# Moving one pair of ScalarE copies from the odd to the even step of a fused GRU and FFN kernel

## The reference

```
gi = x_t @ W_ih + b_ih ; gh = h @ W_hh + b_hh           # 3 gates of 512
r, z = sigmoid(i_r + h_r), sigmoid(i_z + h_z)
n = tanh(i_n + r * h_n) ; h = (1 - z) * n + z * h       # 64 steps in sequence
qx, sx, sc = quantise(h[:, up_index])                   # row max, scale, round to FP8
t = silu(qx @ Wg.T * ...) * (qx @ Wu.T * ...)           # 1408 columns
qt, st, sct = quantise(t) ; y = qt @ Wd.T * ...
out = x + y
```

## Time and profile before

| | |
|---|---|
| median of the runs | 2902.66 us |
| the profiled execution | 2908.95 us, its span 2907.2 us |
| TensorE (PE) busy | 2569.9 us, 88% |
| VectorE (DVE) busy | 1682.8 us, 58% |
| GpSimd (POOL) busy | 1240.1 us, 43% |
| ScalarE (ACT) busy | 1141.0 us, 39% |
| mean granted TensorE clock | 0.960 of full speed |

### The profile page before, as it was taken

One profiled execution on the slowest core, in us unless ns is written; L12 is line 12 of the kernel. 1 busy time (PEld: TensorE's weight loads), 2 busy tenths in 40 slices (PEclk: granted clock), 3 DMA queues, 4 the chain that ended last, 5 costly groups with the idle time before them and its releaser, 6 DMA issues. The chain is left out here.

```text
span 2907.2 us, 154632 instructions
## 1 busy us (share of the span) xinstructions
PE 2569.9 (88%) x67605; PEld 1678.1 (58%) x67605; DVE 1682.8 (58%) x3398; ACT 1141.0 (39%) x2317; POOL 1240.1 (43%) x598
## 2 busy tenths in 40 slices
PE   2088999999889999998999999999996999999995
PEld 1066777776768888886664564745542444444442
DVE  8852222226622222226628778877483888888886
ACT  1312222225622222225603333323233777777773
POOL 0255666662156666662160450704501333333333
PEclk8599999999999999999999999999997999999997
DMA  6833222224422222226463352443522232322321
GB/s 192 237 84 79 73 70 73 73 73 116 129 62 72 71 73 71 71 73 174 135 155 113 99 161 85 137 147 95 165 93 91 66 93 80 94 83 86 91 57 51
DMA packets 234843, 293.74 MB, mean 101 GB/s; under 512 B 69581, under 2 KB 194023, under 8 KB 233895
## 3 DMA queue, kind: packets, MB, share of 16 engines
q1 hardware_dynamic: 212743, 240.84, 29.6%
q10 hardware_dynamic: 18304, 36.19, 3.6%
q0 software_dynamic: 3680, 15.21, 1.8%
HBM read 231.61 MB, written 60.45 MB: 100 GB/s over the span
## 5 line engine op out<-in xcount | busy, mean ns | idle before, releaser
L1145 PE MATMUL psum<-second_shared 64*32 64x384 f16 x32768 | 1026.9, 324 | 52.3 <-issue 33.8
L1153 PE MATMUL psum<-low_w,low_hot 64*32 64x384 f16 x16384 | 758.7, 324 | 3.2 <-issue 3.2
L1372 DVE TENSOR_SCALAR second_shared<-psum 32x384 f16<-32x384 f32 x496 | 272.3, 549 | 747.7 <-PE psum L1145 740.4
L953 POOL TENSOR_TENSOR low_hot<-first_shared,sum_mask 128x1024 f16<-128x1024 f16 x256 | 500.4, 1955 | 468.8 <-DVE first_shared L1359 196.1
L1145 PEld LDWEIGHTS psum<-second_shared 64*32 64x32 f16 x32768 | 562.7, 93 | 201.5 <-issue 94.6
L947 POOL TENSOR_TENSOR second_shared<-first_shared,whole_mask 128x2048 f16<-128x2048 f16 x128 | 462.7, 3615 | 456.1 <-PE psum L1145 346.0
L1044 ACT ACTIVATE second_shared<-psum 32x384 f16<-32x384 f32 x496 | 239.8, 483 | 800.3 <-PE psum L1145 794.4
L1233 PE MATMUL psum<-low_w,low_hot 64*64 64x384 f16 x12288 | 515.5, 326 | 16.8 <-issue 11.1
L1233 PEld LDWEIGHTS psum<-low_w,low_hot 64*64 64x64 f16 x12288 | 374.6, 108 | 152.8 <-issue 17.2
L310 PE MATMUL psum<-w_x,x_cols 128*64 128x512 f32 (+1 forms) x1856 | 310.8, 493 | 9.4 <-ACT x_cols L280 9.4
L1153 PEld LDWEIGHTS psum<-low_w,low_hot 64*32 64x32 f16 x16384 | 283.7, 93 | 57.9 <-issue 5.0
(11 more groups left out here) (286 smaller groups left out, 2722.7 us busy)
## 6 DMA issues: line engine op xcount, KB each, us to landing
low_w<-w_rows SPq DMA_DIRECT2D x384, 144.0 KB
low_w<-w_rows SPq DMA_DIRECT2D x256, 120.0 KB
second_shared<-w_rows SPq DMA_DIRECT2D x1024, 24.0 KB, 1.8
x_gates<-x_out ACTq DMA_DIRECT2D x58, 384.0 KB, 2.3
xg<-x_gates SPq DMA_DIRECT2D x58, 384.0 KB, 3.2
low_w<-w_rows SPq DMA_DIRECT2D x256, 72.0 KB
low_w<-w_rows SPq DMA_DIRECT2D x384, 48.0 KB
w_rows<-quantised SPq DMA_DIRECT2D x24, 384.0 KB, 4.7
```

Of the source, the lines that this page charges most:

```text
L953: nc.gpsimd.tensor_tensor(low_hot[:, buf].rearrange("p (s k) b -> p s k b", s=SUBS), low_a[:, slot, bass.ds(c, 1), :, :].rearrange("p a s ...
L1145: last = nc.tensor.matmul(run[m][u][j * Q:(j + 1) * Q, :], whole_hot[rows[u], m, sign, kk, j % 2 * Q:(j % 2 + 1) * Q], whole_w[rows[u], m, ...
L1153: nc.tensor.matmul(run[m][u][j * Q:(j + 1) * Q, :], low_hot[rows[u], m, kk, j % 2 * Q:(j % 2 + 1) * Q], low_w[rows[u], m, at:at + UC], sta ...
L1372: last = nc.vector.tensor_scalar(whole_w[u * B:u * B + Q, m, 0, bq, :], run[m][u][bq * Q:(bq + 1) * Q, :], 1.0 / HIGH_ONE, None, ALU.mult)
```

## The change

`state_values` is called in the first part of `tile_work` (even step) rather than in the second (odd step). There it is the first thing, ahead of `t_copy` and `t_value`, and it takes tile t+1: the same tile that was taken one step earlier, at the end of pair t-1. The call for tile 1 ahead of the loop goes, since pair 0 now makes it. No instruction is added or dropped.

```diff
                     def tile_work(t):
+                        if live(t + 1):
+                            state_values(t + 1)
                         if live(t - 2):
                             t_copy(t - 2)
                         if live(t - 1):
@@
                         if live(t + 1):
                             state_copy(t + 1)
-                        if live(t + 2):
-                            state_values(t + 2)
                         yield
@@
                     copy_state(0)
                     state_values(0)
                     state_copy(0)
-                    state_values(1)
```

## The result

| | before | after |
|---|---|---|
| median of six runs | 2903.22 us | 2888.11 us (2883.72 to 2889.74) |
| ratio, with its 95% interval | | 0.9941 (0.9929 to 0.9953) |
| the profiled execution | 2908.95 us | 2889.74 us, its span 2887.9 us |

The change makes the kernel 0.59% faster, between 13.6 and 20.6 us. The two medians of the table differ by 15.1 us, a ratio of 0.9948, inside that interval; 16.6 us were forecast. In the kernel after, the lines from `copy_state(0)` on lie one lower than before: L2166 is L2165 now, L2340 is L2339.

A forecast was written before the change was run, and what follows sets the result against it. TensorE was taken to bound the kernel, idling in 28 even steps because ScalarE's sigmoid released `rhn` late. 14.6 us plus 2.0 us made 16.6 us off 2902.7, giving 2886.1 us, range 2881 to 2893.

The forecast's parts named there:

- What bounds: Plain stage: TensorE is busiest, only its gaps can shrink; in 28 of 58 steps `rhn` waits for ScalarE's late sigmoid.
- The term of 28 x 0.52 = 14.6 us: Even steps: sigmoid starts earlier, `rhn` then waits for TensorE, gaining 0.52 us in each of 28 steps.
- The pause at a table load: ScalarE ahead of the sigmoid's table load: a pause would leave 2886.7, or 2889.5 with 1.38 us of drain; 3%.
- The term of 22 x 0.09 = 2.0 us: Loop's even steps: with `hm` gone from beside zh, `rhn` to `h` falls from 1.92 to 1.83 us in 22 pairs.
- The cover in the even step: ScalarE's 2.17 us of idling before `val` takes in the moved 1.34 us, with 0.83 left.
- the prediction's first rival: Even step: `val` moves back by the whole 1.34 us, the odd sigmoid is late, 6.2 us stay, 2896.5; 7%.
- Start and end, the clock: First and last steps give nothing; the second pair's slow matmuls could give back 0 to 1.5 us, taken as 0.
- The profiled execution and the median: Whole kernel: the runs' median lies 6.3 us below the profiled execution, put down to profiling, untouched by the edit.
- The low end: Range's lower limit, 2881: 2884.6 with the clock up, as much again for the kernel's end, 0.6 for spread.

The follow-up runs named there:

- e1: Kernel before with only the second instruction of `state_values` (`hvb`) moved to the even step, `hv` left in the odd step: 2884.88 us, 0.9939 of before.
- e3: Kernel before with only GpSimd's order changed, `hm` put behind the residual's addition: 2902.30 us, 0.9997 of before.
- e4: Kernel after with VectorE's wait for the stored state moved from ahead of `h` to the start of the step: 2884.04 us, 0.9937 of before.
- e2: Kernel after with `state_values` placed last in the even step, behind `val` and `vb`: 3014.76 us, 1.0391 of before.
- e6: Kernel after with TensorE's `gate_up` wait cut in two, one per bank, and VectorE's stored-state wait at the step's start: 2864.77 us, 0.9874 of before.

## Why the prediction was right

The forecast was 2886.1 us and the median is 2888.1, with the reason that it gave, but not with all of its terms. With the one wrong term at nothing the sum would have been 2888.1 as well; that it agrees to the last figure is luck, since the runs of the kernel after lie 6 us apart.

- **What bounds.** Right. The even `rhn` waited for the sigmoid, the sigmoid for ScalarE. After the change all 58 `rhn` wait for TensorE. e1 gets the same 26 pairs with half of the move, and in e3 the other effect that was expected of the change, GpSimd leaving zh alone, doesn't move `h`.
- **The term of 28 x 0.52 = 14.6 us.** Right: 0.52 us for each of the 26 pairs, 13.6 us in all. The table load ran at once behind `state_copy` and ahead of the gate, and `q` stayed 0.44 us ahead of `rhn`.
- **The pause at a table load.** It did not come: in the kernel after the load follows `state_copy` by 0.01 us, and in e1 the sigmoid starts 1.32 us after the copy ahead of the load ends (2398.52 to 2399.84). The 1.38 us of drain that the Trainium skill, "ScalarE: Activation LUTs", section "What ACT_TABLE_LOAD costs", adds to the load are not there in this trace; the measurement decides. In e1 the sigmoid starts 4.75 us after the even `state_part` (2395.09 to 2399.84) against 3.70 in the kernel after, and the pairs are as long: a pause of 1 us would have cost next to nothing.
- **The term of 22 x 0.09 = 2.0 us.** Wrong. "With `hm` gone from there I expect the odd step's 1.83" came out as 1.92 still, and the even step is 0.52 us shorter and not the 0.6 forecast. The step failed by putting a difference between even and odd steps down to the neighbour that could be seen, zh beside GpSimd. zh did fall to 0.42 us, but it was not the last that `h` waited for. e4 shows the wait ahead of `h` in its place: with it at the start of the step 1.82 us were left. The rows could have said so: the written-out pairs, which I left out of the term, had a `rhn` to `h` of 1.83 us with GpSimd beside zh as well (2265.16 to 2266.99 in the third pair before).
- **The cover in the even step.** Right: 0.96 us of ScalarE's idle time left where 0.83 were forecast; `hm` and the addition ended at 2559.46, before `state_round`. e2 shows that the place within the even step matters: behind `val` and `vb` the same move ends 112 us above the kernel before. What the prediction's first rival would cost, `val` itself moved back by 1.34 us, no run shows.
- **Start and end, the clock.** The second pair's slow matmuls are gone (13.11 us from its even to its odd step before, 11.03 after), but the third pair's `state_part` took 6.55 us in place of 5.38. The 0 that I took was near by luck: from the first `state_part` to the third pair's odd step the profiles, whatever their order, took 53.4 to 58.5 us.
- **The profiled execution and the median.** Wrong: the 6.3 us between them were put down to profiling itself. The kernel after was profiled at 1.6 us above its median, and the profiled executions of e1 (2882.68) and e6 (2859.85) are the fastest of their kernels. The sum did not use the 6.3 us.
- **The low end.** Its terms give 2884.6 - 1.5 - 0.6 = 2882.5 and not the 2881 that it states. The measured time lies above both.

## What to carry to other kernels

Where two engines release the same instruction, the gain from making one earlier ends where the other one releases it: read that moment first, and move only as much as reaches it. A piece of work can be put where its engine idles for another engine's result, if what waits for that piece still gets it in time. If it doesn't, the loss can be far larger than the gain: 112 us in e2, against 15 us gained. After a gap is closed, look for the next wait on the same chain: here it was a wait for two buffers where each half needed one, worth more than the change itself (17.2 and 13.6 us over the same 26 pairs).

## What was not expected

- The first five steps of the plain stage took 58.26 us in the kernel before and 54.81 in e3, whose sigmoids and matmuls are in the same order; over all profiles they took 53.4 to 58.5 us. Windows of the second and third pair up to the odd step (granted clock is the third figure from the end) in the kernel before and in e3:

```profile
2236.18:2270.70 34.52, 28.45 (x158) 12.09 (x157) 24.59 (x48) 22.28 (x36) 10.54 (x8) 0.95 0.22 67
```

```profile
2234.43:2267.31 32.88, 26.82 (x158) 11.72 (x157) 24.57 (x48) 23.44 (x38) 10.80 (x8) 1.00 0.25 71
```

  The clock falls for a few matmuls somewhere in these pairs (to 0.53 in the earlier trace rows) in some executions and not in others. The time up to the first `state_part` differs as well, 2204.5 to 2212.5 us over the profiles, in code that no kernel here changes. Both are of the size by which the runs of one kernel differ; how much of that each makes was not measured.
- VectorE's operations with two inputs from the on-chip memory (L2246, L2249) took 1.64 us beside GpSimd and 0.69 alone, while those that read a gate bank (`rhn`) or one input only (L2292, 1.62 us in the kernel after with `hm` beside it) did not change. In e2 they don't look slowed but held up: 57 times one of them lay beside one of GpSimd's single operations, and each time it ended 0.54 to 0.56 us after that operation had ended. zh, in the kernel before, ended 0.27 to 0.32 us after `hm` in all 27 steps in which they overlap.
- A wait in the loop's body ahead of `h` cost 0.09 us on VectorE that the written-out form of the same wait did not; there about as much (0.08 us) is lost between `h` and the next `state_part`, and why was not tested.
